# A graph layer on one core: who fetches gathered rows for five groups, and which queue issues the place transfers

## The reference

```python
h = jnp.maximum(_layernorm(x, axis=-1), 0.0)
p1 = jnp.tanh(h @ pp_W1 + pp_b1) @ pp_W2 + pp_b2
inter = jnp.concatenate([p1[src], p1[dst]], axis=-1)
inter = (inter @ pi_W1 + pi_b1) @ pi_W2 + pi_b2
inter = (inter @ pi_W3).reshape(E, 64, 8)
i1 = jnp.einsum('ecb,eb->ec', inter, edge_attr_8)
i1 = jnp.tanh(i1 @ ii_W1 + ii_b1) @ ii_W2 + ii_b2
out = x + segment_sum(i1, dst, 6250)
```

## Time and profile before

| | |
|---|---|
| Median of 3 runs | 1979.13 us (1978.99 to 1981.69) |
| The profiled execution's own time | 1983.09 us |
| Its span, first to last instruction | 1981.2 us |
| Mean granted TensorE clock | 0.963 of full speed |
| Busy: TensorE, VectorE, ScalarE, GpSimd | 87%, 73%, 56%, 75% of the span |

### The profile page before, as it was taken

How to read it: one execution, slowest core, us unless ns; L and a number is a source line. 1 busy time by engine, 2 the same in 40 slices (tenths; PEclk the granted TensorE clock), 3 DMA queues, 4 the chain that set the end, 5 groups by cost and what they waited for, 6 DMA issues and landing times.

```text
span 1981.2 us, 58993 instructions
## 1 busy us (share of the span) xinstructions
PE 1733.1 (87%) x20012; PEld 1134.5 (57%) x20012; DVE 1449.0 (73%) x1939; ACT 1109.5 (56%) x2419; POOL 1479.1 (75%) x1569
## 2 busy tenths in 40 slices
PE   7699999989988898888888888888888888888998
PEld 6466566655555555555555555555555555555666
DVE  7688778877677777677777777677777767777766
ACT  5666656655555555555555555555555555555554
POOL 7777777777777777777777777777777777777773
PEclk9799999999899999999999999899999999999999
DMA  6543333333333332332333323333233233332331
GB/s 141 115 82 62 67 67 64 61 65 66 58 63 58 62 66 56 63 62 56 62 55 61 62 56 60 61 63 64 55 63 62 56 59 62 59 59 54 59 71 44
DMA packets 266170, 127.83 MB, mean 65 GB/s; under 512 B 188169, under 2 KB 238328, under 8 KB 265864
## 3 DMA queue, kind: packets, MB, share of 16 engines
q1 hardware_dynamic: 214767, 74.86, 17.9%
q0 software_dynamic: 49664, 50.96, 15.4%
q10 hardware_dynamic: 1558, 0.15, 0.1%
HBM read 119.42 MB, written 6.00 MB: 63 GB/s over the span
## 4 chain that ended last, share of the span: by engine, by line
POOL 62%; issue 21%; PE 11%; ACT 2%; DMA 1%; SPq 1%; DVE 1%; ACTq 0%; DVEq 0%; POOLq 0%
POOL u_rows L568 62%; PE bank L1379 5%; PE bank L1474 1%; PE bank L1362 1%; DMA loc_bc<-loc_tab 1%; PE bank L1386 1%; PE spread_ps L1371 1%; DVE o_sb L987 1%; PE bank L1346 1%; ACT st_sb L756 0%; SPq L472 0%; SPq L440 0%; PE spread_ps L1208 0%; PE bank L1356 0%; DMA v_tab<-acc_all 0%
## 5 line engine op out<-in xcount | busy, mean ns | idle before, releaser
L568 POOL DMA_INDIRECT u_rows<-u_tab,src_e x1424 | 1352.4, 950 | 434.1 <-issue 433.1
L987 DVE TENSOR_TENSOR o_sb<-st_sb,spread_ps 128x2048 f32<-128x2048 f32 x391 | 892.9, 2284 | 365.0 <-PE spread_ps L1371 346.8
L756 ACT ACTIVATE st_sb<-bank,s_bias 64x256 f32<-64x256 f32 x1564 | 734.3, 469 | 438.0 <-PE bank L1362 406.9
L1379 PE MATMUL bank<-o_sb,g_sb 128*64 128x256 f32 x6256 | 807.0, 403 | 1.0 <-DVE o_sb L987 0.8
L1379 PEld LDWEIGHTS bank<-o_sb,g_sb 128*64 128x64 f32 x6256 | 433.5, 143 | 232.9 <-issue 36.7
L1362 PE MATMUL bank<-ident,u_rows 128*128 128x128 f32 x1436 | 259.3, 304 | 191.9 <-DMA u_rows<-u_tab,src_e 191.0
L1051 DVE TENSOR_TENSOR hot_t<-loc_bc,bank 126x512 bf16<-126x512 bf16 x391 | 268.8, 688 | 144.0 <-PE bank L1474 59.7
L1362 PEld LDWEIGHTS bank<-ident,u_rows 128*128 128x128 f32 x1436 | 189.8, 192 | 240.5 <-DMA u_rows<-u_tab,src_e 228.0
L1474 PEld LDWEIGHTS bank<-hot,t_sb 128*65 128x65 f32 x3128 | 216.1, 139 | 158.6 <-issue 150.6
L744 ACT ACTIVATE tt_sb<-bank,z_bias 128x256 f32<-128x256 f32 x391 | 185.4, 474 | 175.1 <-PE bank L1379 174.4
L1474 PE MATMUL bank<-hot,t_sb 128*65 128x42 f32 x3128 | 262.8, 235 | 9.1 <-DVE acc_all L1100 8.6
(11 more groups left out here) (148 smaller groups left out, 353.3 us busy)
## 6 DMA issues: line engine op xcount, KB each, us to landing
loc_bc<-loc_tab SPq DMA_DIRECT2D x391, 126.0 KB
u_rows<-u_tab,src_e POOLq DMA_INDIRECT x1424
sp_stage<-u_tab SPq DMA_DIRECT2D x1344, 0.2 KB
v_win<-v_tab SPq DMA_DIRECT2D x391, 15.8 KB
basis<-edge_attr SPq DMA_DIRECT2D x24, 256.0 KB, 4.2
v_tab<-acc_all SPq DMA_DIRECT2D x6, 336.0 KB
basis<-u_tab,src_e POOLq DMA_INDIRECT x100, 2.7
u_tab<-basis SPq DMA_DIRECT2D x6, 224.0 KB
```

Source lines behind the costliest of these rows:

```text
L568: pool.indirect_dma_start(out=u_rows[:, g % UR, j, :] if g >= AHEAD else first_u[:, g - XG, j, :], out_offset=None, in_=u_tab[:, :], in_of ...
L756: last = nc.scalar.activation(tiles[h * D:(h + 1) * D, j], s_ps[part].rearrange("p (q a e) -> p q a e", q=2, a=TILES), ACT.Identity, bias= ...
L987: return nc.vector.tensor_tensor(o_sb[:, r, :, :].rearrange("p c (j e) -> p j c e", j=TILES), st_sb[:, r, :].rearrange("p (j e) -> p j e", ...
L1379: last = nc.tensor.matmul(z_ps[h * D:(h + 1) * D, 0:2 * P], g_sb[:, c, :], o_sb[:, r, c, 2 * h * P:(2 * h + 2) * P], start=(c == 0), stop= ...
```

## The change

The places at which SP fetches change, and so does the way it does so. There are five groups now, 83, 157, 231, 305 and 380, and the last group, 390, goes to GpSimd. Each is fetched in 74 steps, and the stretches follow each other without a gap from step 4 to step 373. In each step SP issues seven row DMAs (one in the last step of a group). It loads indices eight at a time, whenever a row number divides by eight, so 64 times in a group. The staged group is put in its place by one DMA and no longer by four. The issue of `loc_bc` for groups from 4 on leaves SP for ScalarE, which issues it for group n+4 behind its copies of step n. TensorE's loop is cut at the five groups and no longer at two. GpSimd waits for the last piece of indices before group 390.

```diff
-    BY_SP = [(135, 4, P), (263, 132, P), (NG - 1, 260, PART)]
+    ROWS = 7
+    BY_SP = [(83, 4), (157, 78), (231, 152), (305, 226), (380, 300)]
+    AT_ONCE = 8
...
-            def fetch_rows(k, p):
-
-                _, at = nc.values_load_multi_w_load_instructions(
-                    sp_idx[p:p + 1, k * TILES:(k + 1) * TILES], engines=[mybir.EngineType.SP], min_val=0, max_val=N - 1,
-                    skip_runtime_bounds_check_because="src names nodes of x")
-                for j in range(TILES):
-                    sp.dma_start(sp_stage[p:p + 1, k % 2, j, :], u_tab[bass.ds(at[j], 1), :]
+            def fetch_rows(k, rows, at):
+
+                for r in rows:
+                    p, j = divmod(r, TILES)
+                    if r % AT_ONCE == 0:
+                        _, at = nc.values_load_multi_w_load_instructions(
+                            sp_idx[0:1, k * GE + r:k * GE + r + AT_ONCE], engines=[mybir.EngineType.SP], min_val=0,
+                            max_val=N - 1, skip_runtime_bounds_check_because="src names nodes of x")
+                    sp.dma_start(sp_stage[p:p + 1, k % 2, j, :], u_tab[bass.ds(at[r % AT_ONCE], 1), :]
                                  ).then_inc(sp_rows_in[k], 16)
...
-                g, _, n = BY_SP[k]
-                sp.wait_ge(sp_rows_in[k], 16 * TILES * n)
-                for j in range(TILES):
-                    sp.dma_start(u_rows[:, g % UR, j, :], sp_stage[:, k % 2, j, :]).then_inc(fetched[k], 16)
+                g, _ = BY_SP[k]
+                sp.wait_ge(sp_rows_in[k], 16 * GE)
+                sp.dma_start(u_rows[:, g % UR, :, :], sp_stage[:, k % 2, :, :]).then_inc(fetched[k], 16)
...
                     if g >= VR:
-                        sp.wait_ge(hot_t_ready, g - VR + 1)
-                        load_loc(g)
                         sp.wait_ge(s_ready, g - VR + 1)
...
-                        if 0 <= g - first_at < n:
-                            fetch_rows(k, g - first_at)
+                        if first_at <= g:
+                            at = fetch_rows(k, range(ROWS * (g - first_at), min(ROWS * (g - first_at + 1), GE)), at)
...
+                    if g == FULL:
+                        pool.wait_ge(last_in, 32)
...
+            def load_loc(g):
+                act.wait_ge(hot_t_ready, g - VR + 1)
+                act.dma_start(loc_bc[0:3 * W, g % VR, :], loc_tab[g:g + 1, :].to_broadcast([3 * W, GE])
+                              ).then_inc(loc_in[g % VR], 16)
...
                     if has(n) and n < TURN:
                         make_s(n)
+                    if has(n + VR):
+                        load_loc(n + VR)
                     if has(n - 2):
                         make_t(n - 2)
```

More of the change, by code:

```diff
@@ L119, in program @@
         sp_stage = sb("sp_stage", [P, 2, TILES, D])
-        sp_idx = sb("sp_idx", [P, len(BY_SP) * TILES], i32)
+        sp_idx = sb("sp_idx", [1, len(BY_SP) * GE], i32)
         v_win = sb("v_win", [3 * W, VR, D], bf16)
@@ L428, in load_sp_idx @@
             def load_sp_idx():
-                for k, (g, _, n) in enumerate(BY_SP):
-                    sp.dma_start(sp_idx[0:n, k * TILES:(k + 1) * TILES],
-                                 src[g * GE:g * GE + n * TILES].rearrange("(p j) -> p j", j=TILES)
+                for k, (g, _) in enumerate(BY_SP):
+                    sp.dma_start(sp_idx[0:1, k * GE:(k + 1) * GE], row(src[g * GE:(g + 1) * GE])
                                  ).then_inc(sp_idx_in, 16)
-            def fetch_rows(k, p):
-                _, at = nc.values_load_multi_w_load_instructions(
-                    sp_idx[p:p + 1, k * TILES:(k + 1) * TILES], engines=[mybir.EngineType.SP], min_val=0, max_val=N - 1,
-                    skip_runtime_bounds_check_because="src names nodes of x")
-                for j in range(TILES):
-                    sp.dma_start(sp_stage[p:p + 1, k % 2, j, :], u_tab[bass.ds(at[j], 1), :]
+            def fetch_rows(k, rows, at):
[6 more added lines that the diff above has]
+                    sp.dma_start(sp_stage[p:p + 1, k % 2, j, :], u_tab[bass.ds(at[r % AT_ONCE], 1), :]
                                  ).then_inc(sp_rows_in[k], 16)
+                return at
             def place_fetched(k):
-                g, _, n = BY_SP[k]
-                sp.wait_ge(sp_rows_in[k], 16 * TILES * n)
-                for j in range(TILES):
-                    sp.dma_start(u_rows[:, g % UR, j, :], sp_stage[:, k % 2, j, :]).then_inc(fetched[k], 16)
+                g, _ = BY_SP[k]
+                sp.wait_ge(sp_rows_in[k], 16 * GE)
+                sp.dma_start(u_rows[:, g % UR, :, :], sp_stage[:, k % 2, :, :]).then_inc(fetched[k], 16)
             def store_early(lo, hi):
@@ L469, in _ @@
                 load_sp_idx()
+                at = None
                 for g in range(NG):
@@ L492, in _ @@
                         sp.wait_ge(sp_idx_in, 16 * len(BY_SP))
-                    for k, (of, first_at, n) in enumerate(BY_SP):
+                    for k, (of, first_at) in enumerate(BY_SP):
                         if k >= 2 and g == first_at:
                             sp.wait_ge(s_ready, BY_SP[k - 2][0] + 1)
-                        if 0 <= g - first_at < n:
-                            fetch_rows(k, g - first_at)
+                        if first_at <= g:
+                            at = fetch_rows(k, range(ROWS * (g - first_at), min(ROWS * (g - first_at + 1), GE)), at)
                         if g == of - 3:
@@ L560, in _ @@
                     k = g // PIECE
+                    if g == FULL:
+                        pool.wait_ge(last_in, 32)
                     if g % PIECE == 0:
                         pool.wait_ge(ld[k % LD], ld_count(k))
-                    if g in [of for of, _, _ in BY_SP]:
+                    if g in [of for of, _ in BY_SP]:
                         continue
@@ L1409, in y_late @@
                     last.then_inc(y_ps, 1)
-            skipped = [of for of, _, _ in BY_SP]
+            skipped = [of for of, _ in BY_SP]
             def step(n, u, first, last_pass, g=None, fetched_pass=False, gone=(0,) * UN):
@@ L1436, in newest @@
                         if fetched_pass and n + u in skipped:
-                            pe.wait_ge(fetched[skipped.index(n + u)], 16 * TILES)
+                            pe.wait_ge(fetched[skipped.index(n + u)], 16)
                         else:
@@ L1495, in _ @@
                 at = AHEAD
-                for of in skipped[:-1]:
+                for of in [of for of in skipped if of < LOOP_END]:
                     with pe.Fori(at, of // UN * UN, UN) as n:
@@ L1504, in _ @@
                     at += UN
-                with pe.Fori(at, LOOP_END, UN) as n:
-                    for u in range(UN):
-                        step(n, u, False, False, gone=gone)
+                if at < LOOP_END:
+                    with pe.Fori(at, LOOP_END, UN) as n:
+                        for u in range(UN):
+                            step(n, u, False, False, gone=gone)
                 for n in range(LOOP_END, NG + 5, UN):
@@ L1510, in _ @@
                         step(n, u, False, True, fetched_pass=True, gone=gone)
+                        if n + u in skipped:
+                            gone[u] += 1
                 pe.wait_ge(acc_done, NG)
```

## The result

The changed kernel took 2095.97 us in the median of 4 runs (2092.97 to 2097.83), the kernel before 1980.41: a ratio of 1.0581, with a 95% interval of 1.0563 to 1.0600. It is 5.8% slower, inside my range of 2012 to 2118, and my 2061 us were 35 us too low. The profiled execution took 2097.83 us, with a span of 2096.0.

A forecast was written before the change was run, and what follows sets the result against it. GpSimd bounds the kernel before; SP's queue becomes the bound at 5.12 us a step. Group 374 reaches ScalarE at 1972.6, plus 76 and 15.1 gives span 2063.7, so 2061 us, 4.1% slower; range 2012 to 2118.

The forecast's parts named there:

- The step: SP's mean fetching step: 4.39 us before, -0.37 loc_bc, +1.20 rows, -0.12 index loads, 0.02 collisions, so 5.12 (5.0 to 5.3).
- Loading eight costs what loading four does: SP's index loads: 0.86 us each with gaps whatever the count, -0.12 us a step; rival of twice the cost, chance 0.03.
- The rival that a load costs by its registers: SP's index loads, set against the sixteen-index run: 0.1 us a register, so no step change and 2096 us; no chance given.
- `loc_bc` off SP: SP's fetching step: the transfer's 0.32 us and 0.05 gap leave, counting in full, -0.37 us a step.
- Collisions: SP and ScalarE issuing at once: 0.02 us a step, within 0 to 0.2; rival of steps 5.25 and over, chance 0.12.
- ScalarE's issue costs nothing: ScalarE's issue of loc_bc, 0.54 to 0.61 us behind its copies: taken as zero, at most 4 us in the last steps.
- GpSimd's two groups: GpSimd's gathers, 381 groups to 379: 10.0 us less if GpSimd stays the bound, worth nothing with SP as bound.
- GpSimd's wait at group 40: GpSimd waits about 12 us for group 32 to be placed, then stays eight groups ahead of TensorE.
- The way into the last stretch: From SP's issue of v_win for group 374 to ScalarE's copy of that group: 5 us.
- the stretch 76: Copies of groups 374 to 390, where SP fetches nothing and TensorE sets the pace: 76 us, bounds 66 and 81.
- the rest 15.1: From the start of the last group's copies to the end of the span: 15.1 us, unchanged from before.
- The break-even of 4.90 us: SP step at which the time stays as before; rival that SP fits under GpSimd, 1965 to 1969 us, chance 0.08.

The follow-up runs named there:

- 4.95: The changed kernel with the eight bounds checks behind each load of window starts left out: 2001.34 us, ratio 1.0108 to the kernel before.
- 5.58: The changed kernel with loc_bc issued by SP again: 2238.03 us, ratio 1.1263 to the kernel before.
- 5.60: The changed kernel with four indices a load in place of eight: 2226.1 us in one execution.
- 4.80: The changed kernel with sixteen indices a load and unchecked window starts, still five groups and seven rows: 1973.94 us, ratio 0.9966 to the kernel before.

## Why the prediction was right, and where it was off

The mechanism is as I had it: SP's step passes GpSimd's 5.0 us, SP becomes the bound from step 4 to step 373, GpSimd loses its lead, and TensorE waits for `v_win`. Five kernels with steps from 4.95 to 5.58 us lie within 4 us of the one line, and the place where it turns over was seen from both sides. For three of them (5.58, 4.95 and 5.60, which came out as 5.56) the step was worked out before the run; with sixteen indices a load I had 4.84 and it was 5.04.

- **The step: 5.12 predicted, 5.21 measured.** This term was mis-sized, and 0.09 x 370 = 33 us are nearly the whole of the error (2063.7 to 2096.0 in span). Laid end to end, from the start of each piece to the start of the next, the rows took 1.74 us of a step before (windows 20 to 80) and 3.03 after: +1.28 where I had +1.20. The index loads took 0.83 and 0.74: -0.09 where I had -0.12. So the price of a row is most of it. I took 0.41 us from clean neighbouring rows. A row behind another row does take 0.42 in the mean in both kernels, but behind an index load it takes 0.49 before and 0.46 after, and right behind a window's DMA, where 298 rows of the changed kernel stand, 0.51. The mean of before, 0.435, would have given 0.07 of the missing 0.08, and was to be had from that trace.
- **Loading eight costs what loading four does: wrong, and hidden by its place.** The two rows that I compared differ in more than their count. The four indices came behind a window's DMA, where a load takes 0.25 us longer; the eight starts came behind a row. At the same place, behind a row, four take 0.56 and eight 0.78. In the change 270 of 320 index loads stand behind rows, so the error and the shift of place cancelled. That was luck: had all stood behind windows, at 1.04, 0.2 us a step and some 80 us would have been missing from my sum (an estimate from these rows). The rival that a load costs by its registers was half right: the time does grow with them, from 0.56 us for four to 2.13 for thirty-two, but by 56 ns each.
- **`loc_bc` off SP: 0.37 us a step.** Right: putting it back adds 0.37.
- **Collisions: 0.02.** Not seen. Rows cost the same 0.437 us with and without ScalarE's issues, and a window with its register instructions 0.96 and 0.95.
- **ScalarE's issue costs nothing.** Right, and cheaper than my 0.54 to 0.61: its median is 0.31 us, and it lies beside the first copy. Timeline of ScalarE in the changed kernel:

```profile
379.27 0.47 ACT L760 ACTIVATE st_sb<-bank,s_bias 64x256 f32<-64x256 f32 x1 [1.01 <-PE bank L1373]
379.28 0.31 ACTq L766 DMA_DIRECT2D loc_bc<-loc_tab  x1
379.75 1.43 ACT L760 ACTIVATE st_sb<-bank,s_bias 64x256 f32<-64x256 f32 x3
381.50 0.47 ACT L748 ACTIVATE tt_sb<-bank,z_bias 128x256 f32<-128x256 f32 x1 [0.31 <-PE bank L1390]
```

The tanh starts 0.31 us behind the copies, as before. The idle time ahead of the copy is 1.01 us, where it was 0.50: that is SP's lateness, seen from here.

- **GpSimd's two groups: worth nothing here.** Right. When the fetches are gone they and the end are worth 16 us.
- **GpSimd's wait at group 40: 12 us.** It was 19.3. Window 32 went out at 223.6 us and not at 216.6, since the steps were longer than I took them and its own, of 7.98 us, held a load of eight starts; it was placed 4 us later, as I had it. This changes nothing in the sum.
- **The way into the last stretch 5 us, the stretch 76, the rest 15.1.** Measured 6.4, 73.4 and 15.3: in sum 1 us off.
- **The break-even of 4.90 us.** By the measured 168.2 it is (1981.2 - 168.2) / 370 = 4.90 too. At 4.95 the kernel was 1.1% slower, at 4.80 (steps 4 to 80) it was 0.3% faster.

## What to carry to other kernels

A queue that only issues has no busy time in the profile, so its room is to be read from a stretch in which nothing holds it: start to start, divided by the steps. Add up there what is moved onto it, at the mean price of an instruction and not at the price in a clean run, and compare with the pace of the present bound; here 0.31 us above the break-even, 370 times over, were 115 us. When a helper fills up, look first at what it does besides the help (checks, small loads, other transfers): leaving out eight checks in every eighth step was worth 95 us here and loading sixteen indices at a time 63, where the help itself brought 16 with its cost taken away.

## What the runs showed of the hardware

- A load of registers on SP took 0.34 us and 56 ns for each index, from 4 to 32 of them (medians 0.56, 0.78, 1.24 and 2.13 us), where most loads follow a row DMA; right behind the DMA of a window it took 0.25 us more (1.04 beside 0.78 for eight, 0.81 beside 0.56 for four).
- The two instructions of a check cost 0.26 us for each value, 2.1 us for eight (2.94 us with them, 0.82 without).
- A row DMA of 256 bytes with its two register instructions took SP 0.42 us in the mean behind another row and 0.51 right behind the DMA of a window.
- ScalarE's sequencer issued a DMA of 126 rows in 0.31 us while the engine ran the first of the four copies in front of it. SP's issue of the same transfer takes 0.32 and stands in full in its step.
